# The second layer norm taken into the down projection of a transformer layer, half of the token tiles at a time, on eight cores of a Trainium2

## What is computed

```python
x = _layernorm(x + attn(x), axis=-1)
g = jnp.einsum('th,ih->ti', xf, gate_w) * gate_s
u = jnp.einsum('th,ih->ti', xf, up_w) * up_s
hdn = jax.nn.silu(g) * u
out = jnp.einsum('ti,hi->th', hdn, down_w) * down_s
x = _layernorm(x + out, axis=-1)
```

## Time and profile before

| | us |
|---|---|
| median of 2 runs | 2035.48 (2032.87 to 2038.1) |
| profiled execution | 2033.44 |
| its span on the slowest core | 2031.9 |
| down projection, first to last matmul | 1630.9 to 1941 |
| second layer norm | 1941 to 2031.9 |

### The profile page before, as it was taken

The page is one execution under the profiler, slowest core; times in us unless marked ns, Lnnn a source line. Parts: engine busy times, 40 slices in busy tenths (PEclk is TensorE's granted clock), DMA queues, the critical chain, the costliest instruction groups (busy, mean ns, idle before and its releaser), DMA issues. The chain is left out here.

```text
span 2031.9 us, 19267 instructions; the slowest of 8 cores (1994.5 to 2031.9 us)
## 1 busy us (share of the span) xinstructions
PE 1440.7 (71%) x7854; PEld 767.8 (38%) x7854; DVE 335.4 (17%) x419; ACT 168.8 (8%) x214; POOL 189.1 (9%) x198
## 2 busy tenths in 40 slices
PE   1676659954554433460599999999999689999920
PEld 0222224411222111120244444444444278888810
DVE  0000001011443333331011111111111100000045
ACT  0110001100110111100010110100100000000011
POOL 1010000001000000012011111111111000000000
PEclk9888779975787666785799999999999799999965
DMA  8744475046002111217777877877877698655076
GB/s 111 98 61 59 67 104 83 1 93 113 31 11 73 63 72 73 73 62 132 95 73 73 83 73 73 83 74 72 83 77 70 74 140 122 103 86 84 30 234 270
DMA packets 296226, 175.45 MB, mean 86 GB/s; under 512 B 201692, under 2 KB 283848, under 8 KB 291017
## 3 DMA queue, kind: packets, MB, share of 16 engines
q0 software_dynamic: 258208, 106.96, 45.8%
q1 hardware_dynamic: 37930, 67.25, 10.4%
HBM read 247.60 MB, written 29.36 MB: 136 GB/s over the span
## 5 line engine op out<-in xcount | busy, mean ns | idle before, releaser
L748 PE MATMUL gups<-x1T,gstr 128*128 128x512 bf16 x1408 | 320.1, 381 | 61.9 <-DMA x1T<-x1bd 61.9
L831 PE MATMUL dnps<-dstr,hT 128*128 128x256 bf16 x2816 | 309.6, 274 | 14.5 <-DMA dstr<-dTd 14.5
L758 PE MATMUL gups<-x1T,ustr 128*128 128x512 bf16 x1408 | 318.3, 379 | 0.0
L831 PEld LDWEIGHTS dnps<-dstr,hT 128*128 128x128 bf16 x2816 | 276.4, 98 | 49.0 <-issue 16.1
L748 PEld LDWEIGHTS gups<-x1T,gstr 128*128 128x128 bf16 x1408 | 138.1, 98 | 230.1 <-issue 65.3
L758 PEld LDWEIGHTS gups<-x1T,ustr 128*128 128x128 bf16 x1408 | 137.8, 98 | 166.1
L341 PE MATMUL kps<-xch,wk_sb 128*128 128x512 bf16 x512 | 122.6, 404 | 79.7 <-DMA xch<-xT 39.8
L773 DVE SCALAR_TENSOR_TENSOR hT<-gups,us_col,silu 128x512 bf16<-128x512 f32 x88 | 66.1, 751 | 602.5 <-PE gups L758 602.5
L476 PE MATMUL scps<-kT,qsT 128*128 128x512 bf16 x256 | 74.2, 444 | 119.6 <-DVE scores L485 115.6
L547 PE MATMUL zpn<-vv,aT_sb 128*128 128x512 bf16 x256 | 74.6, 450 | 75.8 <-DVE aT_sb L536 75.8
L359 PE MATMUL vps<-wv_sb,xch 128*128 128x512 bf16 x512 | 113.6, 383 | 12.0 <-DMA wv_sb<-wvT 12.0
(11 more groups left out here) (96 smaller groups left out, 572.2 us busy)
## 6 DMA issues: line engine op xcount, KB each, us to landing
gstr<-gTd POOLq DMA_DIRECT2D x44, 512.0 KB, 7.0
ustr<-uTd POOLq DMA_DIRECT2D x44, 512.0 KB, 8.9
dstr<-dTd POOLq DMA_DIRECT2D x8, 2816.0 KB, 22.9
xch<-xT POOLq DMA_DIRECT2D x8, 2048.0 KB, 23.3
wq4b<-wq POOLq DMA_DIRECT2D x16, 512.0 KB, 9.8
masks<-msk SPq DMA_DIRECT2D x8, 1024.0 KB, 7.6
Pq<-prj POOLq DMA_DIRECT2D x16, 512.0 KB, 6.2
xqp<-xq SPq DMA_DIRECT2D x32, 256.0 KB, 4.4
```

The costliest lines, as they stand in the source:

```text
L748: (lambda bi, tch, gsl, ct: lambda e: e.matmul(gups[:, gsl, :], gstr[bi][:, ct, :], x1T[:, ct, tch*512:(tch+1)*512], start=(ct == 0), stop ...
L758: (lambda bi, tch, usl, ct: lambda e: e.matmul(gups[:, usl, :], ustr[bi][:, ct, :], x1T[:, ct, tch*512:(tch+1)*512], start=(ct == 0), stop ...
L831: (lambda bi, ts, ps, it: lambda e: e.matmul(dnps[ps][:, 0:256], hT[:, it, ts*128:(ts+1)*128], dstr[bi][:, it, :], start=(it == 0), stop=( ...
```

## The change

- The token tiles are taken in two halves. For each half, all eight weight blocks are loaded and used for four tiles. So there are 16 loads in place of 8, each for four groups of 44 matmuls in place of eight. The number of matmuls, evictions and stores is the same.
- There are two weight buffers in place of three.
- The second layer norm is a function of one tile, `plan_ln2`, and is listed for the four tiles of a half directly behind the half's down projection, so four tiles stand between the two halves and four behind the second. The barrier and the stage of its own are gone.
- In `plan_ln2` the sum is read into `outs` and the residual into `rx`, the add and the scaling work in place in `outs`, mean and variance are worked out for one tile by five small operations on GpSimd, and the output write is listed at the end of each tile, ahead of the reads of the next.

The diff, with the unchanged middle of the removed stage cut:

```diff
--- before.py
+++ after.py
@@ -787,11 +787,13 @@
             with esE:
                 sE = lambda n, sh, dt: esE.enter_context(nc.sbuf_tensor(n, sh, dt))
                 dstr = [sE("dstr0", [128, IT, 256], BF16),
-                        sE("dstr1", [128, IT, 256], BF16),
-                        sE("dstr2", [128, IT, 256], BF16)]
+                        sE("dstr1", [128, IT, 256], BF16)]
                 ffns = sE("ffns", [128, 2, 256], F32)
                 ds_b = sE("ds_b", [128, D], F32)
                 dsrow = sE("dsrow", [1, D], F32)
+                rx = sE("rx", [128, 2, D], F32)
+                outs = sE("outs", [128, 2, D], F32)
+                sqscr2 = sE("sqscr2", [128, D], F32)
                 dnps = [esE.enter_context(nc.psum_tensor("dnps0", [128, 512], F32)),
                         esE.enter_context(nc.psum_tensor("dnps1", [128, 512], F32))]
                 dspp = esE.enter_context(nc.psum_tensor("dspp", [128, 512], F32))
@@ -813,123 +815,135 @@
                          [("pe", mpk)], [("ve", 1)])
                     pp_free = B.m("ve")
                 mv_dsb = B.m("ve")
-                dstr_free = [0, 0, 0]
+                dstr_free = [0, 0]
                 dn_free = [0, 0]
                 fst = [0, 0]
-                for dc8 in range(8):
-                    bi = dc8 % 3
-                    sd = "sd%d" % bi
-                    md = B.dma("gpsimd",
-                               (lambda dc8, bi: lambda e: e.dma_start(
-                                   out=dstr[bi][:], in_=dT_r[:, :, dc8*256:(dc8+1)*256]))(dc8, bi),
-                               sd, [("pe", dstr_free[bi])])
-                    for ts in range(8):
-                        ps = (dc8 * 8 + ts) % 2
-                        sff = "sff%d" % ps
-                        for it in range(IT):
-                            B.op("tensor",
-                                 (lambda bi, ts, ps, it: lambda e: e.matmul(
-                                     dnps[ps][:, 0:256], hT[:, it, ts*128:(ts+1)*128],
-                                     dstr[bi][:, it, :],
-                                     start=(it == 0), stop=(it == IT-1)))(bi, ts, ps, it),
-                                 [(sd, md), ("ve", dn_free[ps])] if it == 0 else (),
-                                 [("pe", 1)] if it == IT-1 else ())
-                        mp_d = B.m("pe")
-                        B.op("vector",
-                             (lambda dc8, ps: lambda e: e.scalar_tensor_tensor(
-                                 out=ffns[:, ps, :], in0=dnps[ps][:, 0:256], scalar=1.0,
-                                 in1=ds_b[:, dc8*256:(dc8+1)*256],
-                                 op0=OP.mult, op1=OP.mult))(dc8, ps),
-                             [("pe", mp_d), (sff, fst[ps]), ("ve", mv_dsb)],
-                             [("ve", 1)])
-                        mv_f = B.m("ve")
-                        dn_free[ps] = mv_f
-                        B.dma("sync",
-                              (lambda dc8, ts, ps: lambda e: e.dma_start(
-                                  out=ffn_r[ts][:, dc8*256:(dc8+1)*256],
-                                  in_=ffns[:, ps, :]))(dc8, ts, ps),
-                              sff, [("ve", mv_f)])
-                        fst[ps] = B.m(sff)
-                    dstr_free[bi] = B.m("pe")
-                bar5 = B.bar()
+                ffn_tile_mark = {}
+                r_free = [0, 0]
+                o_free = [0, 0]
+
+                def plan_ln2(ts):
+                    sl = ts % 2
+                    sfr = "sfr%d" % sl
+                    so = "so%d" % sl
+                    sffn, sffv = ffn_tile_mark[ts]
+                    B.dma("sync",
+                          (lambda ts, sl: lambda e: e.dma_start(
+                              out=outs[:, sl, :], in_=ffn_r[ts]))(ts, sl),
+                          sfr, [(sffn, sffv), ("ve", o_free_v[sl]), (so, o_free[sl])])
+                    m2 = B.dma("sync",
+                               (lambda ts, sl: lambda e: e.dma_start(
+                                   out=rx[:, sl, :], in_=x1f_r[ts]))(ts, sl),
+                               sfr)
+                    B.op("vector",
+                         (lambda ts, sl: lambda e: e.tensor_add(
+                             outs[:, sl, :], outs[:, sl, :], rx[:, sl, :]))(ts, sl),
+                         [(sfr, m2)], [("ve", 1)])
+                    B.op("vector",
+                         (lambda ts: lambda e: e.tensor_reduce(
+                             sum8[:, ts:ts+1], outs[:, ts % 2, :], axis=AX.X,
+                             op=OP.add))(ts),
+                         (), [("ve", 1)])
+                    mv_add = B.m("ve")
+                    B.op("scalar",
+                         (lambda ts, sl: lambda e: e.activation(
+                             out=sqscr2[:], in_=outs[:, sl, :], func=AF.Square,
+                             accum_out=sq8[:, ts:ts+1]))(ts, sl),
+                         [("ve", mv_add)], [("se", 1)])
+                    ms_sq = B.m("se")
+                    B.op("gpsimd",
+                         (lambda ts: lambda e: e.tensor_scalar(
+                             out=nmean8[:, ts:ts+1], in0=sum8[:, ts:ts+1],
+                             scalar1=-1.0/D, scalar2=None, op0=OP.mult))(ts),
+                         [("ve", mv_add)], [("ge", 1)])
+                    B.op("gpsimd",
+                         (lambda ts: lambda e: e.tensor_mul(
+                             tmp8[:, ts:ts+1], nmean8[:, ts:ts+1], nmean8[:, ts:ts+1]))(ts),
+                         (), [("ge", 1)])
+                    B.op("gpsimd",
+                         (lambda ts: lambda e: e.tensor_scalar(
+                             out=var8[:, ts:ts+1], in0=sq8[:, ts:ts+1],
+                             scalar1=1.0/D, scalar2=None, op0=OP.mult))(ts),
+                         [("se", ms_sq)], [("ge", 1)])
+                    B.op("gpsimd",
+                         (lambda ts: lambda e: e.tensor_sub(
+                             var8[:, ts:ts+1], var8[:, ts:ts+1], tmp8[:, ts:ts+1]))(ts),
+                         (), [("ge", 1)])
+                    B.op("gpsimd",
+                         (lambda ts: lambda e: e.tensor_scalar(
+                             out=var8[:, ts:ts+1], in0=var8[:, ts:ts+1],
+                             scalar1=float(EPS), scalar2=None, op0=OP.add))(ts),
+                         (), [("ge", 1)])
+                    mg_var = B.m("ge")
+                    B.op("scalar",
+                         (lambda ts: lambda e: e.activation(
+                             out=tmp8[:, ts:ts+1], in_=var8[:, ts:ts+1], func=AF.Ln))(ts),
+                         [("ge", mg_var)], [("se", 1)])
+                    B.op("scalar",
+                         (lambda ts: lambda e: e.activation(
+                             out=rstd8[:, ts:ts+1], in_=tmp8[:, ts:ts+1], func=AF.Exp,
+                             scale=-0.5))(ts),
+                         (), [("se", 1)])
+                    ms_rs = B.m("se")
+                    B.op("vector",
+                         (lambda ts, sl: lambda e: e.tensor_scalar(
+                             out=outs[:, sl, :], in0=outs[:, sl, :],
+                             scalar1=nmean8[:, ts:ts+1], scalar2=rstd8[:, ts:ts+1],
+                             op0=OP.add, op1=OP.mult))(ts, sl),
+                         [("se", ms_rs)], [("ve", 1)])
+                    mv_o = B.m("ve")
+                    o_free_v[sl] = mv_o
+                    B.dma("sync",
+                          (lambda ts, sl: lambda e: e.dma_start(
+                              out=out_r[ts], in_=outs[:, sl, :]))(ts, sl),
+                          so, [("ve", mv_o)])
+                    o_free[sl] = B.m(so)
+
+                o_free_v = [0, 0]
+                for half in range(2):
+                    for dc8 in range(8):
+                        bi = dc8 % 2
+                        sd = "sd%d" % bi
+                        md = B.dma("gpsimd",
+                                   (lambda dc8, bi: lambda e: e.dma_start(
+                                       out=dstr[bi][:],
+                                       in_=dT_r[:, :, dc8*256:(dc8+1)*256]))(dc8, bi),
+                                   sd, [("pe", dstr_free[bi])])
+                        for tsl in range(4):
+                            ts = half * 4 + tsl
+                            ps = tsl % 2
+                            sff = "sff%d" % ps
+                            for it in range(IT):
+                                B.op("tensor",
+                                     (lambda bi, ts, ps, it: lambda e: e.matmul(
+                                         dnps[ps][:, 0:256], hT[:, it, ts*128:(ts+1)*128],
+                                         dstr[bi][:, it, :],
+                                         start=(it == 0), stop=(it == IT-1)))(bi, ts, ps, it),
```

(71 more changed lines are left out.)

29 lines of the change are left out of this document (removed).

## The result

The changed kernel takes 2203.9 us in the median. The ratio to the kernel before is 1.0833, 95% interval 1.0799 to 1.0866. The prediction had 2170 and a range of 2140 to 2212.

The account below looks back on a forecast made before the run. The down projection was taken as bound by TensorE alone. 1630.9 + 170.7 + 108.1 + 170.7 + 86.8 = 2167.2 us of span, +135.3 on before, so 2035.5 + 135 = 2170 us; range 2140 to 2212.

Parts of the forecast that it names:

- slow loads: Rival on the weight loads: with eight cores loading almost without pause, 25 us a block, +40, 2210 us; chance 0.09.
- falling clock: Rival on TensorE: its clock falls at each stall, each block starting at 1.2 GHz, +10, 2181 us; chance 0.14.
- The queues: Between the halves: GpSimd's load waits behind tile 3's variance, VectorE's evictions behind four tiles, SyncE's reads behind the previous write.
- The tile: Second layer norm: tiles do not overlap; reads 8.9 then 10.2 us, operations 10.3; four tiles take 80.7 us.
- The middle: Between the halves, TensorE stands 108.1 us: 1.1 + 80.7 - 2.2 + 28.5 for the first block's load.
- The end: Behind the last matmul: 1.1 + 80.7 + 5.0 make 86.8 us, against 90.9 before.
- The loads: Down projection: 16 loads of 22.9 us, each serving 19.2 us of matmuls; pace 21.4 us, half 170.7, price 29 us.
- the formula for pairs: Weight loads with two buffers: a block is issued when the block two ahead ends, pace (22.9 + 19.2)/2 = 21.05 us.
- The average stall of 2.2 us: TensorE in the halves: argument against clock loss, that at a pace of 21.4 us stalls average 2.2 us.
- The third buffer: Weight buffers: taking the third away costs about nothing, since the pace is that of the transfer.
- The other side: Rival: TensorE goes on through the first half's layer norm, the 108.1 us fall away, 2062 us, 1.3% over before; chance 0.07.

Follow-up runs that it names:

- norm_spread: Changed kernel with the first half's four layer norm tiles worked off under the second half and the last four overlapped; ratio 1.0406 to the kernel before.

## Why the prediction was right, and which terms were off

**The number.** The change costs 168 us where 135 were forecast, 2204 against 2170. The range up to 2212 held because it allowed for the slow loads and the falling clock, which had chances of 0.09 and 0.14 and both came in part; the forecast itself put both at nothing.

**The queues.** The writing out of each engine's order was right in every point. The ninth load is released by the variance of tile 3 (0.66 us behind it), VectorE's hold shows once that load is out of the way (72.2 us), and SyncE's order makes the tile (20.1 us, or 10 to 13 when it is changed).

**The tile.** Forecast 20.5 us, measured 20.1; the whole of four 80.7 against 81.4. The estimate of the reads was what mattered: 8.9 and 10.2 forecast, 8.0 and 9.9 measured. The end was forecast at 86.8 and took 83.8, as its four tiles took 78.4. The forecast counted no load of the activation table; there is one of 1.3 us in the middle.

**The middle.** Forecast 108.1, measured 112.7. The excess is the load: 33.4 us from issue to start in place of 28.5. The tiles took 0.7 more, and the load went out 3.3 us ahead of the last write's issue, where 2.2 had been taken.

**The loads.** This is the term that was mis-sized. The step reads: "Between them lies the pace of loads back to back ... I take 21.4", and "Price of the loads: 2 x 14.7 = 29 us". The halves take 182.1 and 186.3 us, forecast 170.7 each: that is 56 us in place of 29, and 27 of the 30 us by which the span missed. Against the one pass of 310.1 us the two halves cost 58 us where the forecast has 31; in it are 43.4 us of waits, eight of them where some 12 with 25 to 30 us were forecast, and 15.4 us of slower matmuls. Two things were wrong in it.
- The landing time of 22.9 was taken as that of a load as such. For a load issued singly it is 20.5 on a core alone, 22.0 in the kernel before on eight cores (the last five loads of each core, 20.3 to 26.1), and 25.3 once other cores load nearly without a pause. The form of the sum held: the pair of blocks from 1681.42 to 1726.74 lasts 21.4 us to the issue of the next load and 24.0 from there to TensorE's start, where 19.2 and 22.9 stood in the formula for pairs. The rival of slow loads named this, with 25 us a block; the argument against it, that three loads in a row took 21.3 each on all cores, did not carry. Over a half the pace is 182.1/8 = 22.8 us a block in the first and 23.3 in the second. The same division gives 21.3 for the forecast and 23.8 for the rival, so it lies between the two.
- The average stall of 2.2 us was no guide for the clock. The buffers are freed one after the other while TensorE runs, so the stalls fall together on each second block and are 4 to 11 us long; the formula for pairs said so already, with 3.7 at each second block. Behind a wait of 1.3 or 1.4 us a block took 19.37, behind 3.7 it took 20.80 and behind 5.4 21.89; the granted clock in the first 4 to 5 us behind waits of 1.4, 3.7 and 5.4 was 1.00, 0.65 and 0.50. The rival of the falling clock happened, and was sized low: of the 15.4 us the forecast had 2.8 in the start of the second half, so 12.6 in place of 10. That a slower block only uses up the stall holds for the second block of a pair; the first one, if slower, also delays the load that the next wait is for.
The Trainium skill, "TensorE: Matmul & The Clock Gate", section "HAM oscillation", describes a kernel in which each wait for data, of some 3 to 5 us, put TensorE back to the half rate. The rows agree for the waits of 3.7 us and more; behind the 1.3 and 1.4 here and the 2.2 to 2.6 of the one core the clock stayed.

**The third buffer.** "Costs about nothing here, since the pace is that of the transfer": half shown. With eight loads it costs nothing. With 16 the DMA engines are not busy throughout (windows of the changed kernel: the halves; then a stretch of matmuls and a wait behind it; last three numbers: granted clock, DMA share, GB/s):

```profile
1632.50:1814.60 182.10, 161.75 (x1408) 140.91 (x1408) 13.16 (x31) 0.00 (x0) 12.46 (x6) 0.94 0.94 132
...
1927.30:2113.60 186.30, 163.23 (x1408) 141.90 (x1408) 13.17 (x31) 0.00 (x0) 12.46 (x6) 0.92 0.95 127
...
1945.00:1950.00 5.00, 5.00 (x49) 4.49 (x47) 0.57 (x2) 0.00 (x0) 0.00 (x0) 1.00 0.08 26
1972.00:1979.00 7.00, 0.00 (x0) 0.00 (x0) 0.00 (x0) 0.00 (x0) 0.00 (x0) 0.50 1.08 119
```

The mean share over the halves is 0.94 and 0.95, while a load alone ran at 1.21, and there are stretches like 1945 to 1950 at 0.08, in which both buffers are full and nothing can be loaded. A third buffer could use these. It was not tried, and there remains open how much of the 58 us it would return. In the wait from 1972 to 1979 the engines are busy at 1.08 and move 119 GB/s, where the single load of the earlier trace rows moved 169 at 1.21: the packets themselves take longer, and no buffer changes that.

**The other side.** "The middle is free" needed a wait of under 13 us. norm_spread takes it away altogether, and it is 4.1% slower than before all the same, where the rival had 1.3%. So even that case was too kind, by the size of the loads, since overlap puts the layer norm's transfers on top of them.

## What to carry to other kernels

Before a stage is folded into another, write down for every engine the list of what stands behind the first wait, the loads of the next stage above all; four lists gave the 108 us of the middle here. Price a split that reads weights twice at the landing time with other cores loading without a pause, not at that of a load with pauses: a transfer with 15 us of slack says nothing of how it behaves with none. And where the gain sought is a short end, look first at what goes to memory and back: keeping the sums on the chip and the statistics with the evictions took 52 us off the end without touching the loads. When a wait is explained by a late issue, look up the landing of the very load that it waited for: in norm_spread the late load was not that one.

## What the runs showed of the hardware

The load of one block (5.77 MB read, cast to 2.88 MB) lands in 20.5 us (median) with one core at work, in 26.6 and 27.2 with cores 0 and 1, in 26.1 to 27.1 with four and in 25.2 to 27.0 with eight cores. For the loads issued singly the medians are 20.5, 25.3, 26.3 and 25.3 us. The limit is reached with two cores. Landing times understate the rate, since two loads of a core overlap. Two loads issued together were both in after 35.0 us at the start of the run on one core and after 43.8 us in the changed kernel (49.4 in the middle), an estimate of 330 and 263 (234) GB/s of reads a core; over a half, waits and all, the changed kernel reads 8 x 5.77 MB in 182.1 us, 253 GB/s a core. What the limit is, the device memory or the way to it, no run tells.
The Trainium skill, "DMA: Bandwidth & Descriptors", section "Bandwidth", says that the two cores of one memory domain each get roughly half of its bandwidth when both stream, about 358 GB/s each. In kind the rows agree, if cores 0 and 1 are such a pair; the rate was lower here, some 234 to 263 GB/s of reads a core.
I had not expected how the clock takes short waits. In the traces of the nine runs with 16 loads, on all their cores, none of the 40 waits of up to 1.9 us in front of a block made that block slower. All 381 from 3.7 us on (the middle left out) made the next block or two 1.2 to 3.0 us slower. Of the 101 between, 65 did and 36 did not, and not in order of length: in norm_spread a block behind 2.46 us took 21.04 at a granted clock of 0.66, in the changed kernel one on core 2 behind 3.16 us took 19.37 at 1.00.
